# Layer 0's deviations taken from the attention's variances, per-expert waits for the low weights, and a first block made in the drain

## The reference

```python
x = x + xattn(layernorm(x), ctx, ctx, mask, ...)
x = x + attn(layernorm(x), ...)
x = x + ffn(layernorm(x), router_w, router_b, ln_g, ln_b, w1, b1, w2, b2)

def _moe_layer(x, rw, rb, g, b, w1, b1, w2, b2):
    logits = einsum('bsh,he->bse', x, rw) + rb
    probs = softmax(logits); vals, idx = top_k(probs, 2); vals = vals / vals.sum(-1)
    xhat = (x - x.mean(-1)) * rsqrt(x.var(-1) + 1e-5)
    xe = xhat * g + b
    h = gelu(xe @ w1 + b1)            # 128 -> 512 features, for each of 4 experts
    y = h @ w2 + b2                   # 512 -> 128
    return sum over the two chosen experts of comb * (x + y)
```

## Time and profile before

| what | value |
|---|---|
| median of 3 runs | 1383.05 us (1374.69 to 1383.26) |
| the profiled execution's own time | 1380.24 us |
| its span, first to last instruction | 1378.5 us |
| PE busy | 1270.3 us (92%) |
| DVE busy | 1203.2 us (87%) |
| ACT busy | 1128.8 us (82%) |
| POOL busy | 714.0 us (52%) |
| mean granted TensorE clock | 0.970 |

### The profile page before, as it was taken

One profiled execution on the slowest core, in us unless ns is written; L12 is line 12 of the kernel. 1 busy time (PEld: TensorE's weight loads), 2 busy tenths in 40 slices (PEclk: granted clock), 3 DMA queues, 4 the chain that ended last, 5 costly groups with the idle time before them and its releaser, 6 DMA issues. The chain is left out here.

```text
span 1378.5 us, 41462 instructions
## 1 busy us (share of the span) xinstructions
PE 1270.3 (92%) x15611; PEld 966.0 (70%) x15611; DVE 1203.2 (87%) x3492; ACT 1128.8 (82%) x1931; POOL 714.0 (52%) x559
## 2 busy tenths in 40 slices
PE   5898999999997689997889979999999999999998
PEld 3576778777776578954567657777777777776776
DVE  4799989999998678977899979998999999999986
ACT  3598999999996656766899968888888888888886
POOL 7276777777776864542334333344333344444343
PEclk9999999999998679999999999999999999999999
DMA  5985676676663279820000000000000000000000
GB/s 157 240 217 156 191 184 183 188 189 183 191 183 86 49 198 209 216 53 1 2 2 2 2 1 2 2 2 2 2 2 2 2 2 2 2 10 17 10 17 17
DMA packets 196269, 109.41 MB, mean 79 GB/s; under 512 B 89740, under 2 KB 194028, under 8 KB 196076
## 3 DMA queue, kind: packets, MB, share of 16 engines
q1 hardware_dynamic: 122032, 84.65, 22.1%
q10 hardware_dynamic: 74044, 22.17, 7.3%
HBM read 67.62 MB, written 39.03 MB: 77 GB/s over the span
## 5 line engine op out<-in xcount | busy, mean ns | idle before, releaser
L1649 POOL TENSOR_TENSOR gl<-gf,gh 128x1024 f16<-128x1024 f32 x128 | 290.6, 2270 | 461.7 <-ACT gh L1671 461.7
L1666 ACT ACTIVATE gf<-pair,b1c 128x512 f32<-128x512 f32 x512 | 329.5, 680 | 77.1 <-PE pair L1846 76.9
L1863 PE MATMUL pair<-w2p,gh 128*128 128x128 f16 x4096 | 356.9, 219 | 4.3 <-DVE hs L1745 2.6
L1863 PE MATMUL pair<-w2p,gl 128*128 128x128 f16 x2048 | 349.7, 219 | 0.0
L1846 PE MATMUL pair<-xh,w1p 128*128 128x512 f16 x1024 | 328.3, 382 | 7.3 <-DVE w1p L1046 7.3
L405 POOL TENSOR_TENSOR pl<-p,ph 128x1024 f16<-128x1024 f32 x128 | 273.1, 2134 | 116.0 <-ACT ph L462 115.9
L1863 PEld LDWEIGHTS pair<-w2p,gh 128*128 128x128 f16 x4096 | 317.5, 98 | 20.8 <-DVE hs L1745 3.1
L1671 ACT ACTIVATE gh<-gf 128x1024 f16<-128x1024 f32 x256 | 270.6, 1057 | 23.6 <-ACT gf L1666 0.4
L1731 DVE SCALAR_TENSOR_TENSOR gl<-gf,gh 128x1024 f16<-128x1024 f32 x128 | 164.0, 1281 | 42.0 <-ACT gh L1671 41.5
L1863 PEld LDWEIGHTS pair<-w2p,gl 128*128 128x128 f16 x2048 | 200.3, 98 | 0.0
L1846 PE MATMUL pair<-xl,w1p 128*128 128x512 f16 x512 | 195.7, 382 | 0.0
(11 more groups left out here) (252 smaller groups left out, 2458.0 us busy)
## 6 DMA issues: line engine op xcount, KB each, us to landing
KS<-k_parts_dram SPq DMA_DIRECT2D x64, 384.0 KB, 4.5
k_parts_dram<-kh SPq DMA_DIRECT2D x64, 256.0 KB, 3.3
cx<-in_ctx_dram ACTq DMA_DIRECT2D x30, 512.0 KB, 4.7
k_parts_dram<-kl SPq DMA_DIRECT2D x64, 128.0 KB, 3.6
w1p<-in_L_ffn_w_dram SPq DMA_DIRECT2D x8, 512.0 KB, 6.0
w2p<-in_L_ffn_w_dram SPq DMA_DIRECT2D x8, 512.0 KB, 8.0
QS<-q_parts_dram ACTq DMA_DIRECT2D x128, 24.0 KB
K<-k_parts_dram SPq DMA_DIRECT2D x8, 384.0 KB
```

Source lines behind the costliest of these rows:

```text
L1649: pool.tensor_tensor(gl[u.m2][:, 0:h, :], gf[u.m2][:, 0:h, :], gh[u.m2][:, 0:h, :], ALU.subtract).then_inc(d_loP, 1)
L1666: act.activation(gf[u.m2][:, c, :], hb[c][:, :], ACT.Gelu, scale=1.0 / WS, bias=b1c[:, u.step.expert(u.e), c]).then_inc(d_g, 1)
L1863: last = pe.matmul(yb[v.m2][:, t * D:(t + 1) * D], g[:, c, t * P:(t + 1) * P], w2p[:, le, part, c, :].rearrange("p a h -> p (a h)"), start ...
```

## The change

**Deviations of layer 0.** hs = (xs - mean) * rs has variance var * rs * rs, so the inverse deviation that layer 0 needs follows from numbers that the attention's normalisation already has. `expert_scale` makes rsE from them and rrE = rs * rsE, so that `normalise_first` makes `xc` from xs directly. `deviations` and the wait for hs fall away for blocks 0 to 7. `expert_scale` runs in slot (7, 3) for tiles 0 to 23 and in unit (2, 1) for tiles 24 to 31; the attention's own deviations of the last eight tiles move from the drain's end to unit (1, 1) (`late_deviations`).

**First block in the drain.** `xc`, its transposes, `xh` and `xl` of block 0 are made in slots (8, 0) to (8, 2). Both `low_weights` 0 and 1 stand in slot (8, 0).

**hs.** ACT makes tiles 0 to 15 (four in (7, 3), four in (8, 0), four each behind units (0, 3) and (1, 3)); DVE makes 16 to 31 (`attended_late`, four in each of units (3, 1) to (6, 1)).

**Low weights.** DVE splits in units 1 and 3 of steps 1 to 6, where it was 2 and 3. PE's single wait is replaced by waits for each expert in block 0 of every layer.

**Last layer.** The addition of xs moves from behind `normalise` (unit 0) to behind `add_bias` (unit 3), ahead of `weigh`.

```diff
+        SCALED = HEAD + 2 * RSTD_STEPS + 4
+        LATE_R = SCALED + NT - HEAD + RSTD_STEPS
+        LATE_SCALED = LATE_R + RSTD_STEPS + 3
+        def expert_scale(dve, own, base):
+            dve.wait_ge(e_ln, base)
+            dve.scalar_tensor_tensor(vE[:, own], mv3[:, own, 1], 1.0, rs3[:, own], ALU.mult, ALU.mult).then_inc(e_ln, 1)
+            dve.wait_ge(e_ln, base + 1)
+            dve.scalar_tensor_tensor(vE[:, own], vE[:, own], 1.0, rs3[:, own], ALU.mult, ALU.mult).then_inc(e_ln, 1)
+            dve.wait_ge(e_ln, base + 2)
+            inverse_deviation(dve, seed, rsE[:, own], rwE[:, own], rt3[:, own], vE[:, own], e_ln, base + 2)
+            dve.scalar_tensor_tensor(rrE[:, own], rs3[:, own], 1.0, rsE[:, own], ALU.mult, ALU.mult).then_inc(e_ln, 1)
+        def normalise_first(dve, n):
+            dve.wait_ge(e_ln, SCALED if 4 * n + 4 <= HEAD else LATE_SCALED)
+            wait(dve, d_xT, n)
+            for k in range(4):
+                t = 4 * n + k
+                dve.tensor_scalar(xc[:, k, :], xs[:, t, :], mv3[:, t, 0:1], rrE[:, t:t + 1],
+                                  ALU.subtract, ALU.mult).then_inc(d_x, 1)
...
-                                for t in range(8):
+                                for t in range(4):
                                     attended(act, t)
                             if at == (NBLK, 0):
                                 act.activation(warm[:, :], gain[:, 0:1], ACT.Gelu)
+                                for t in range(4, 8):
+                                    attended(act, t)
+                            if at == (NBLK, 1):
+                                tokens_high(act, 0)
                                 high_weights(act, 2)
...
+                            if at == (7, 3):
+                                expert_scale(dve, slice(0, HEAD), HEAD + RSTD_STEPS + 1)
                             if at == (NBLK, 0):
-                                dve.wait_ge(d_hs, 8)
-                                for k in range(8):
-                                    dve.bn_stats(st8[:, k, :], hs[:, k, :]).then_inc(d_ln, 1)
...
+                                normalise_first(dve, 0)
+                                for le in range(2):
+                                    dve.wait_ge(e_b1, le + 1)
+                                    low_weights(dve, le)
+                            if at == (NBLK, 2):
+                                tokens_low(dve, 0)
                     blocks(step, prepare)(dve)
-                    dve.wait_ge(c_st, 2 * NT)
-                    attended_late()
...
+                            if at == (NBLK, 1):
+                                pe.wait_ge(d_x, 4)
+                                pe.wait_ge(c_oc, NT)
+                                for k in range(4):
+                                    last = pe.transpose(bank[6][:, k * P:(k + 1) * P], xc[:, k, :], ident[:, :])
+                                last.then_inc(d_xT, 1)
...
-                        if splits and split and e in split_units:
+                        if split and cur and 1 <= cur.n <= (LE - E) // 2 and e in split_units:
                             split(eng, 2 * cur.n + (E - 2 + split_units.index(e)))
...
-                if ready:
-                    ready()
...
-                    LATER = {(1, 1): (16, 20), (1, 3): (20, 24), (2, 1): (24, 28), (2, 3): (28, NT)}
+                    LATER = {(0, 3): (8, 12), (1, 3): (12, 16)}
...
+                    def attended_late(n):
+                        dve.wait_ge(e_ln, LATE_R if 4 * n + 4 > HEAD else HEAD + RSTD_STEPS + 1)
+                        for t in range(4 * n, 4 * n + 4):
+                            dve.tensor_scalar(hs[:, t, :], xs[:, t, :], mv3[:, t, 0:1], rs3[:, t:t + 1],
+                                              ALU.subtract, ALU.mult).then_inc(d_hs, 1)
...
-                        if u and third and e == 1 and not opening:
+                        if third and e == 1 and third.layer:
                             deviations(third)
...
-                        if opening and e == 2:
-                            deviations(third)
...
                         if u and e == 3:
                             add_bias(u.step)
+                        if u and f and e == 3 and f.layer == L - 1:
+                            blk = slice(4 * f.block, 4 * f.block + 4)
+                            dve.wait_ge(d_x, 4 * f.n + 4)
+                            dve.tensor_tensor(hs[:, blk, :], hs[:, blk, :], xs[:, blk, :], ALU.add).then_inc(d_sum, 1)
                         if at == (0, 1):
                             low_weights(dve, 3)
+                        if at == (1, 1):
+                            late_deviations()
+                        if at == (2, 1):
+                            expert_scale(dve, slice(HEAD, NT), LATE_R)
+                        if u and e == 1 and 3 <= u.step.n < 7:
+                            attended_late(u.step.n + 1)
...
-                    steps(dve, unit, low_weights, (2, 3), lead=True)
+                    steps(dve, unit, low_weights, (1, 3), lead=True)
...
-                        if isinstance(u.n, int) and u.n in (2, 3):
-                            pe.wait_ge(e_lo1, u.n + 1)
+                        if u.step.block == 0:
+                            pe.wait_ge(e_lo1, E * u.step.layer + u.e + 1)
```

More of the change, by code:

```diff
@@ L1060, in build @@
         e_rwh, e_b2, e_ln = sem("e_rwh"), sem("e_b2"), sem("e_ln")
-        st8 = sb(whole, "st8", [P, 8, 6], F32)
-        mv8 = sb(whole, "mv8", [P, 2, 4, 2], F32)
-        rs8, rw8, rt8 = (sb(whole, f"rs8_{i}", [P, 2, 4], F32) for i in range(3))
+        vE, rsE, rwE, rrE = (sb(whole, f"rsE_{i}", [P, NT], F32) for i in range(4))
+        xh = [sb(whole, f"xh{i}", [P, 4 * P], F16) for i in range(2)]
+        xl = [sb(whole, f"xl{i}", [P, 4 * P], F16) for i in range(2)]
         warm = sb(whole, "warm", [P, 1], F32)
@@ L1311, in step @@
                                 act.activation(warm[:, :], gain[:, 0:1], ACT.Gelu)
+                                for t in range(4, 8):
+                                    attended(act, t)
+                            if at == (NBLK, 1):
+                                tokens_high(act, 0)
                                 high_weights(act, 2)
-                            if at == (NBLK, 1):
-                                for t in range(8, 12):
-                                    attended(act, t)
                             if at == (NBLK, 2):
@@ L1526, in _ @@
                     blocks(step)(pe)
-                    pe.wait_ge(d_x, 4)
-                    pe.wait_ge(c_oc, NT)
-                    for k in range(4):
-                        last = pe.transpose(bank[6][:, k * P:(k + 1) * P], xc[:, k, :], ident[:, :])
-                    last.then_inc(d_xT, 1)
                     pe.wait_ge(e_cols, 5)
@@ L1590, in __init__, with steps, run @@
                     self.step, self.e, self.n, self.m2 = step, e, step.unit + e, e % 2
-            def steps(eng, unit, split=None, split_units=(0, 2), ready=None, lead=False):
-                SPLITS = (LE - E) // 2
-                def run(it, c, final, prepare=True, attend=True, splits=False, moments=lead):
+            def steps(eng, unit, split=None, split_units=(0, 2), lead=False):
+                def run(it, c, final, prepare=True, attend=True, moments=lead):
                     cur = Step(eng, it, c) if attend else None
@@ L1620, in steps @@
                 run(0, 0, False)
-                for s in range(1, 1 + SPLITS):
-                    run(0, s, False, splits=True)
-                if ready:
-                    ready()
-                for s in range(1 + SPLITS, NSTEP - 2):
+                for s in range(1, NSTEP - 2):
                     run(0, s, s >= LAST - 1)
@@ L1672, in unit @@
                                                    ACT.Copy).then_inc(d_hi, 1)
-                        if f and e == 1:
-                            act.wait_ge(d_xT, f.n + 1)
+                        if u and f and e == 1:
                             wait(act, d_h, FC * E * (f.n - 1))
-                            act.activation(xh[f.m2][:, :], tbk[:, :], ACT.Copy).then_inc(d_xh, 1)
-                        if f and e == 1 and not u:
+                            tokens_high(act, f.n)
+                        if not u and f and e == 1:
                             high_weights(act, 3)
-                            for t in range(12, 16):
-                                attended(act, t)
                         at = (u.step.n, e) if u and isinstance(u.step.n, int) else None
                         if at in LATER:
-                            if LATER[at][0] == HEAD:
-                                act.wait_ge(e_ln, HEAD + RSTD_STEPS + 1 + NT - HEAD + RSTD_STEPS + 1)
                             for t in range(*LATER[at]):
@@ L1738, in combine @@
                         dve.wait_ge(d_comb, v.step.n + 1)
-                        if final and v.e == 0:
```

(10 more changed lines are left out.)

107 lines of the change are left out of this document (45 added, 62 removed).

## The result

The changed kernel takes 1369.67 us (median of 7 runs, 1368.14 to 1373.39) against 1382.68 for the kernel before (7 runs beside it): ratio 0.9909, 95% interval 0.9894 to 0.9924. That is a gain of 12.6 us where 19.2 were forecast; the time was forecast at 1361.5. The profiled execution of the changed kernel took 1373.39 us, with a span of 1371.6.

The account below looks back on a forecast made before the run. PE was taken to bound the middle of the expert stage, DVE layer 0; terms -4.7 - 3.4 - 1.4 - 3.0 - 7.3 + 0.6 = -19.2 us from 1380.24 gave 1361.0, forecast as 1361.5, range 1351 to 1370.

Parts of the forecast that it names:

- The drain, unit (0, 0): End of attention and first expert unit: PE starts earlier and at full clock, -4.7 us (bounds -3.6 and -5.5).
- step 0 to 1: Layer 0's first step: waits behind `deviations` go, ACT is late next, -3.4 us (bounds -2.6 and -5.4).
- Steps 1 to 6: Layer 0: added DVE work fits its slack; 46.3 us for steps 1 to 3 (-1.4), 67.5 for 3 to 6 (-3.0).
- Rival (a): Layer 0 stays near its old pace through ACT's load and DVE's pair in unit 1; 1367.5 us, chance 0.17.
- Steps 6 to 8: End of layer 0: PE's single wait, worth 9.2 us, goes, DVE work returns; 47.2 us, -7.3 (bounds -5 and -10).
- Steps 8 to 23: Instructions stay the same but for new waits, long met: 0 us.
- The last layer: The moved addition stands still beside POOL's `gl`: +0.1 us a step, +0.6 for the layer.
- (b): The last layer's addition finds a gap and steps run at 22.27 us; about 1355 us, chance 0.12.
- (c): Last layer: DVE's `gl` falls behind POOL's in some steps, +6 to +13 us; 1367 to 1374, chance 0.08.
- (d): DVE's `gl` slips behind POOL's in all layers, making the kernel slower; up to 1406 us, chance 0.04.
- (e): Expert waits fail because a late low weight is met at step 8; 9.2 us stay, 1370 us, chance 0.03.
- cT at 24.2, 23.8 and then 22.5: Expected sign: the once-a-step ACT instruction at 24.2, 23.8 and then 22.5 us a step in layer 0.

Follow-up runs that it names:

- experiment 1: The changed kernel with DVE's low weights in units 2 and 3 again, not in 1 and 3; 1362.30 us, ratio 0.9859.
- (2): The changed kernel with `attended_late` in unit 2, behind route and combine, not in unit 1; 1363.69 us, ratio 0.9876.
- (3): The changed kernel with `attended_late`'s four tensor_scalars replaced by four bn_stats of the same tiles, leaving out half of hs; 1368.27 us, ratio 0.9896.
- experiment 11: The changed kernel, late pieces in unit 0, low weights in units 0 and 2 of steps 3 to 5, 2 and 3 otherwise; 1357.75 us.
- 8: The changed kernel with low weights in units 2 and 3, and the late pieces in unit 0 of steps 1 and 2; 1360.42 us, ratio 0.9842.
- (4): The kernel before with only PE's waits changed, to one per expert in the first block of all layers; 1373.82 us, ratio 0.9937.
- experiment 5: The changed kernel with only step 6's `attended_late` call moved to unit 2, behind combine; 1366.35 us, ratio 0.9877.
- (12): The changed kernel with the last layer's sum of hs and xs put back behind normalise; 1371.50 us, ratio 0.9913.

## Why the prediction was too low

**The drain, unit (0, 0) and step 0 to 1** came as argued, and somewhat larger: -5.35 for -4.7 and -4.25 for -3.4. No run changed them alone; the traces alone bear them out.

**Steps 1 to 6 are the step that failed.** The forecast was 46.3 + 67.5 us, the measurement 50.93 + 71.21. The prediction said of DVE that `attended_late` is at most 1.64 us and "lies in the slack of DVE", and of the two late pieces "where DVE has 3.7 us free: nothing". Three things were wrong with it. It counted slack over a whole step, where the work stands in one leg of a loop, from xl to z, at whose end ACT waits. Moving the pair out of the leg (experiment 1), moving `attended_late` out of it (2) and shortening it (3) each brought steps 3 to 6 from 71.2 to about 69. The last 1.5 us to the forecast's 67.5 belong to another limit, which the prediction didn't have; experiment 11 took 1.1 of them away. It priced the instructions without the stop at POOL's gl, which the prediction itself had read from the earlier trace rows and used for the last layer only: 3.08 us, where its bound was 1.64 and the same four take 1.11 in a gap. And it gave the pair's move to unit 1 no price in steps 1 to 5: 2.2 us each in steps 1 to 3 and 3 to 6 by experiment 1. In steps 1 and 2 the late pieces cost at least a further 1.3 us (8 against 1). Rival (a) had the place, the pair in unit 1, and with 1367.5 came within 2.2 us. That is luck in part: it gave steps 1 to 8 a gain of 5.0, measured was 0.2, and the drain, step 0 and the last layer made up for it. What it said of ACT's load did not hold, since ACT was busy 21.27 of 23 us (740 to 763) in experiment 1's kernel too, at the faster pace.

**Steps 6 to 8.** The barrier was worth 8.2 us (4), against 9.2. The forecast let deviations and `attended_late` take 2.7 of the possible 10; in the changed kernel 4.1 of the 8.2 were lost again, most of it by a stop of xc and a lower clock behind it, and experiment 5 took 3.1 of that away.

**Steps 8 to 23** are 0 as forecast. **The last layer** was right in mechanism: the sum takes 2.08 us beside POOL's gl, and from that gl's end to xl it is 8.05 us where it was 8.18 before. DVE and POOL there:

```profile
1233.62 2.08 DVE L1841 TENSOR_TENSOR hs<-hs,xs 128x512 f32<-128x512 f32 x1
...
1233.01 2.14 POOL L1653 TENSOR_TENSOR gl<-gf,gh 128x1024 f16<-128x1024 f32 x1 [3.35 <-ACT gh L1675]
```

A step came out at -0.14, not +0.1. The rest of the -2.58 the prediction didn't have: 0.6 in the first step, which goes with the place of the sum (12), and the slip. No run explains either. Rivals (b), (c) and (d) did not occur, nor did (e). Of the list in the prediction, the full clock in the first unit (1.00 from 632 to 642), the first gelu at about 628 (633.04 - 5.62 = 627.4), no idle time for the low weights at step 7 and the long sum came true; cT at 24.2, 23.8 and 22.5 did not (23.39, 25.24, 23.7), and steps of 23.5 and more in layer 0 were named as the sign of being wrong. One sum in it is off: the strong bounds add up to -27.2, not -26.

## What to carry to other kernels

Slack of an engine over a step says nothing of a place in it: draw the loop that sets the pace (who waits for this queue's next result, who waits for theirs), and charge what is moved to the leg it lands in and to the next deadline behind it. The same 4 us of pieces gave 57.6, 48.7 or 47.4 us for two steps, by the unit in which they stood. A price found for a stop in one place (VectorE beside GpSimd) is to be tried on every other term in which the same kind of instruction meets the same neighbour.
